# Perceiver block on one core: the last rows' normalisation ahead of the choice of experts, and clock-keeping products moved into two other waits

## What is computed

```python
x = x + xattn(layernorm(x), ctx_768)      # 16 heads, 257 context rows of 192 numbers a batch
x = x + local_attention(layernorm(x))     # each row attends to its neighbours at distance <= 2
x = x + experts(layernorm(x))             # 8 experts, each row goes to one
```

```python
router_logits = x @ Wr + br
expert_mask = one_hot(argmax(router_logits, axis=-1), 8)
for e in range(8):
    h = gelu(x @ W1[e] + b1[e])           # 256 to 1024
    h = gelu(h @ W2[e] + b2[e])           # 1024 to 512
    y = h @ W3[e] + b3[e]                 # 512 to 256
    out = out + expert_mask[:, e:e + 1] * y
```

## Time and profile before

| | |
|---|---|
| median of 3 runs | 704.46 us (704.05 to 704.51) |
| the profiled execution | 707.72 us |
| its span, first to last instruction | 706.0 us |
| TensorE busy | 686.0 us (97%) |
| VectorE busy | 473.8 us (67%) |
| ScalarE busy | 450.7 us (64%) |
| GpSimd busy | 437.7 us (62%) |
| mean granted TensorE clock | 0.992 |
| slices of 17.65 us in which TensorE is busy less than 90% | the first, the 24th and 25th (406 to 441 us), the last |

### The profile page before, as it was taken

One profiled execution on the slowest core, in us unless ns is written; L12 is line 12 of the kernel. 1 busy time (PEld: TensorE's weight loads), 2 busy tenths in 40 slices (PEclk: granted clock), 3 DMA queues, 4 the chain that ended last, 5 costly groups with the idle time before them and its releaser, 6 DMA issues.

```text
span 706.0 us, 26647 instructions
## 1 busy us (share of the span) xinstructions
PE 686.0 (97%) x9297; PEld 582.1 (82%) x9298; DVE 473.8 (67%) x1456; ACT 450.7 (64%) x1071; POOL 437.7 (62%) x596
## 2 busy tenths in 40 slices
PE   7999999999999999999999968999999999999996
PEld 6888888888888888888888756888888888888885
DVE  4467677777777777777798878999961991259001
ACT  4656666666766766666666644575757576666663
POOL 6475665655656565656555663677766776767553
PEclk9999999999999999999999997999999999999999
DMA  7432233333323333343458334239033541272100
GB/s 214 118 89 78 75 76 96 91 88 82 97 67 80 102 90 78 81 97 80 94 136 268 99 109 169 90 100 330 25 106 112 176 147 45 82 229 69 40 7 1
DMA packets 56178, 74.35 MB, mean 105 GB/s; under 512 B 6589, under 2 KB 41950, under 8 KB 56128
## 3 DMA queue, kind: packets, MB, share of 16 engines
q1 hardware_dynamic: 49792, 60.63, 31.2%
q0 software_dynamic: 2992, 8.26, 3.8%
q10 hardware_dynamic: 3344, 4.80, 1.9%
HBM read 67.30 MB, written 7.27 MB: 106 GB/s over the span
## 4 chain that ended last, share of the span: by engine, by line
PE 93%; DVE 2%; DMA 1%; issue 1%; POOL 1%; ACT 1%; SPq 0%; POOLq 0%; ACTq 0%; DVEq 0%
PE ps_s L2046 18%; PE ps_kv L1623 12%; PE ps_kv L1631 11%; PE ps_p L1709 8%; PE ps_o L1695 6%; PE ps_s L1642 6%; PE ps_p L1994 5%; PE ps_kv L1994 4%; PE ps_o L2060 4%; PE ps_s L2025 3%; PE ps_m L1828 2%; PE ps_m L1774 2%; PE ps_m L1747 2%; PE ps_m L1832 2%; PE ps_s L2054 1%
## 5 line engine op out<-in xcount | busy, mean ns | idle before, releaser
L877 ACT ACTIVATE prob<-prob,neg_max 128x257 f32<-128x257 f32 x256 | 111.2, 501 | 42.2 <-DVE neg_max L1122 40.6
L1122 DVE CUSTOM_DVE_ANT_0 prob<-ps_s,mask_add 128x257 f32<-128x257 f32 x256 | 94.7, 421 | 64.3 <-PE ps_s L1642 64.2
L1582 DVE CAST w<-w_raw 128x512 fp32r<-128x512 f32 x94 | 68.1, 725 | 57.1 <-DMA w_raw<-in_L_ffn_W_dram 57.1
L1585 DVE TENSOR_TENSOR w<-w_raw,w 128x512 fp32r<-128x512 f32 x112 | 103.1, 923 | 3.6
L685 POOL TENSOR_TENSOR ctx_parts<-ctx_raw,ctx_parts 128x512 fp32r<-128x512 f32 x64 | 82.9, 1295 | 23.8 <-ACT ctx_parts L872 21.9
L2046 PE MATMUL ps_s<-w,h_hi 128*128 x368 | 90.5, 397 | 0.0
L1631 PE MATMUL ps_kv<-wkv_hi,ctx_parts 128*128 128x256 f32 x512 | 84.6, 293 | 0.2 <-ACT kT L881 0.2
L1623 PE MATMUL ps_kv<-ctx_parts,wkv_hi 128*128 128x256 f32 x512 | 84.2, 292 | 0.3 <-POOL ctx_parts L685 0.2
L885 ACT COPY v<-ps_kv 128x512 f32<-128x512 f32 x64 | 37.5, 586 | 70.3 <-PE ps_kv L1631 70.3
L698 POOL COPY last_prob<-prob 128x4 f32<-128x4 f32 x64 | 12.3, 192 | 112.1 <-ACT prob L877 108.4
L813 POOL TENSOR_TENSOR h_lo<-h,h_hi 128x512 fp32r<-128x512 f32 x46 | 64.2, 1397 | 27.6 <-ACT h_hi L1017 21.4
(11 more groups left out here) (307 smaller groups left out, 1513.6 us busy)
## 6 DMA issues: line engine op xcount, KB each, us to landing
w_raw<-in_L_ffn_W_dram SPq DMA_DIRECT2D x24, 1024.0 KB, 7.2
ctx_raw<-in_ctx_turned_dram SPq DMA_DIRECT2D x63, 256.0 KB, 3.5
mask_add<-mask_dram SPq DMA_DIRECT2D x64, 128.5 KB, 3.4
w_raw<-in_L_ffn_W_dram SPq DMA_DIRECT2D x8, 512.0 KB, 4.0
rows_dram<-x3n ACTq DMA_DIRECT2D x15, 256.0 KB, 4.3
xt<-in_x_dram SPq DMA_DIRECT2D x16, 128.0 KB, 2.1
xr<-in_x_dram SPq DMA_DIRECT2D x16, 128.0 KB, 2.3
slot_x<-rows_dram,slot_ids POOLq DMA_INDIRECT x23, 4.0
```

Source lines behind the costliest of these rows:

```text
L877: a.activation(prob[:, g, :], prob[:, g, :], ACT.Exp, bias=neg_max[:, g:g + 1], scale=-1.0).then_inc(exp_done, 1)
L1122: d.tensor_tensor_reduce(prob[:, r, :], ps_s[r][:, 0:J], mask_add[:, k, :], -(HD ** -0.5), 3.0e38, ALU.add, ALU.min, neg_max[:, r:r + 1]). ...
L1582: d.tensor_copy(w[:, b, HI, part], raw[:, b, part]).then_inc(rounded, 1)
L1585: last = d.tensor_tensor(w[:, b, LO, part], raw[:, b, part], f32(w[:, b, HI, part]), ALU.subtract)
```

## The change

VectorE issues the normalisation of the last tile's rows directly behind the scaled logits, ahead of the choice of the expert, where it stood behind the choice. On TensorE the clock-keeping transposes behind the bias transpose become 20 instead of 5, five new ones stand between the counts and the last chunk sum, and those behind the product that finds the slots' tokens become 16 instead of 24: 41 in these places where there were 29. Nothing that is computed changes.

```diff
--- before.py
+++ after.py
@@ -1517,13 +1517,13 @@
                 match_single(2)
                 dve.wait_ge(raw_logits_done, 2)
                 scale_logits(t).then_inc(tail_taken, 1)
+                normalise(2, t, x3n[:, 0:D], x3n[:, D:2 * D], xn3_done)
 
             last_tile()
 
 
             dve.wait_ge(tail_taken, taken("logits"))
             choose_single(3)
-            normalise(2, TILES - 1, x3n[:, 0:D], x3n[:, D:2 * D], xn3_done)
             rank_single(3, ps_m[:, E:2 * E])
             totals = ps_m[:, 2 * E:3 * E]
             d.tensor_scalar(padded[:, :], totals, 1.0, float(P - 1), ALU.max, ALU.add).then_inc(route, 1)
@@ -1961,14 +1961,15 @@
                 pe.wait_ge(bias_in, 32)
                 n_b = E * (F1 + F2) // P
                 t.transpose(ps_s[3][:, 0:n_b], bias_rows[:, :], ident[0:n_b, 0:n_b]).then_inc(bias_turned, 1)
-                keep_clock(5)
+                keep_clock(20)
                 fill_chunks(2, 3, 4, 14)
                 rank_single(3, ps_m[:, E:2 * E])
                 count_all(ps_m[:, 2 * E:3 * E]).then_inc(ranked, 1)
+                keep_clock(5)
                 fill_chunks(15).then_inc(chunks_filled, 1)
                 pe.wait_ge(route, 7)
                 t.matmul(ps_kv[:, 0:SLOTS], chunk_tokens[:, :], of_slot[:, :], start=True, stop=True).then_inc(tokens_found, 1)
-                keep_clock(24)
+                keep_clock(16)
 
             last_tile()
```

## The result

| | before | changed |
|---|---|---|
| median of 9 runs | 704.51 us (704.04 to 706.15) | 706.58 us (703.95 to 707.73) |
| ratio of the times, 95% interval | | 1.0023 [1.0013, 1.0033] |
| the profiled execution (its span) | 707.72 us (706.0) | 706.0 us (704.3) |

The changed kernel is 0.23% slower, about 1.6 us, and scatters more.

The account below looks back on a forecast made before the run. It took TensorE, 93% of the chain, as the bound, so a gather shift counts one for one. Gather −0.48 plus clock +0.12 gave −0.36 us on the median 704.46: 704.1 us, range 703.1 to 705.2.

Parts of the forecast that it names:

- The normalisation ahead of the choice: VectorE, last tile: normalising directly behind the logits lands the rows sooner, so the first gather starts 0.48 us earlier.
- The 0.13 us that the insertion was to cost the ids: VectorE, choice of expert: the inserted normalisation makes `top`, the ranking and the ids 0.13 us later.
- The first rival (the ids hold it): First gather: it waits for the slots' ids, not the rows, so it starts 0.13 us later; 704.6 us, chance 0.32.
- The transposes ahead: TensorE before the ids: 20 and five transposes fit in existing waits, cost nothing; clock 1.00 in 421 to 422.
- the 16 in place of 24 and the clock: TensorE behind the ids' product: 16 transposes end at 426.1 or 427.3, within the gather wait; no clock gain counted.
- No instruction waits for them: TensorE behind the ids' product: the clock-keeping transposes lie in the wait for the gather and hold up nothing.
- I expect the lower level for layer 1 again: Layer 1 of slot 0: the clock is low again, so work starting 0.48 us earlier gives back 0.12 us.
- if the next six take more than 2: Sign of being wrong: the six products of layer 1's second half take more than 2 us.
- TensorE idle for 3 to 4 us: Before layer 1: with 16 transposes TensorE idles 3 to 4 us instead of 1.6.
- The price of a transpose at the lower level: TensorE behind the ids' product: 24 transposes in 4.65 us, so 0.19 us each at the lower clock.
- the clock comes back later: Layer 1, second half: low clock costs +1.5 us, with the gather unimproved +0.13; 706.1 us, chance 0.08.
- Putting the difference on the median: Whole kernel: durations came from the 707.72 us profiled execution, but the −0.36 us was applied to the 704.46 us median.

Follow-up runs that it names:

- the late store: Kernel before with 20 transposes instead of 5 behind the bias transpose and five new ahead of the last chunk sum, normalisation unmoved, expert number bounded: 1.0031 of before, 707.26 us.
- control: Kernel before plus only an assertion bounding the expert number that TensorE loads, an edit all variants carry: 1.0002 of before, 704.73 us.
- the filled kernel: Changed kernel, expert number bounded, transposes filling every wait (32, 10, 3, 32 behind the ids' product, 4 before layer 1): 0.9991 and 0.9986 of before, 704.29 and 704.18 us.

## Why the prediction was wrong

It said 704.1 us, 703.1 to 705.2, and gave slower by over 0.2% a chance of 0.07. It came out 0.23% slower, with a median of 706.58 us.

**The normalisation ahead of the choice** was right and somewhat better than costed: the gather came 0.59 us earlier (forecast 0.48). The 0.13 us that the insertion was to cost the ids was 0.02: `top` came 0.21 us later relative to the logits (0.54 against 0.33), but `chosen_single` lasted 0.24 us in place of 0.40. That the rows, not the ids, held the gather is shown by seven profiles with the edit (issue at 4.61 to 4.63) against six without it (5.20 to 5.22), and by the one with the late store (6.73). Where the edit is absent the gather starts 0.83 to 0.86 us after the store has landed, whether that is at 424.38 (control) or at 426.3 (the late store). The first rival (the ids hold it) is out.

**The transposes ahead** cost nothing on TensorE, as I said, and kept the clock full in 421 to 422. That 20 more of them are 40 instructions on TensorE, which are fetched through the same DMA engines as the rows, I did not count. In the changed kernel it does no harm, because the store has landed by 422.75 and the packet comes at 424.4; with the transposes alone the gather starts 1.5 us later (6.73 against 5.20).

**The step that failed is the one on the 16 in place of 24 and the clock.** "No instruction waits for them" was wrong: in the control the 24 are in the chain, and slot 0's transposes wait 0.6 us behind them. And "I expect the lower level for layer 1 again", priced at 0.12 us, took the lower level in the first profile for the kernel's ordinary state. It was not: in the control layer 1 runs at full clock, so there was 2.4 us to lose, and with 16 the kernel loses part of it in most runs: 2.32 and 2.08 us for the two halves in the changed kernel's profile, where the control has 1.65 and 1.40. The recorded sign of being wrong, "if the next six take more than 2", is what came.

The wait itself was mis-sized too. The prediction had TensorE idle for 3 to 4 us (its own terms give 2.6 to 3.8), since it took over the 5.00 us of the first profile's gather. The gather took 3.5 us, the idle time was 0.97 and 1.22 us in the two profiles, and the lower level came all the same. The price of a transpose at the lower level, 0.19 us, was the mean of 24 of which the last ran at full clock; with all but the last few at the lower level they took 5.21 us in the control, 0.22 each.

The rival "the clock comes back later" had the direction and half of the mechanism: the second half of layer 1 does run partly at the lower level (2.08 us). Its sum, 706.1 us, is close to what was measured, but by luck. It counted 1.5 us in the second half alone and a gather that had not improved; measured were 0.7 us in each half and a gather 0.6 us earlier, from a starting point 2.6 us lower. I gave it 0.08 with the argument that "little is left to lose". That argument was read off one execution.

**Putting the difference on the median** was the same fault: the text noted that the profiled execution was 3.26 us above it and did not ask where. Of that, 2.6 us lay in the very passage that was to be changed. With layer 1 at full clock as the starting point, a lower level through both halves is +2.4, and slot 0's transposes, which no longer stand behind the 24, start 0.9 earlier (8.22 against 9.10): slower by 1.5 us, where 1.6 was measured. That sum was made after the fact, and that it fits so well is luck in part: the changed kernel's two profiles lose 0.6 and 1.7 us in the passage against the control.

## What to carry to other kernels

Before costing a change to a passage, hold the profiled execution against the median of the runs: if it is some microseconds off, find where, since the state it shows may be the exception and the terms read from it have the wrong sign. Products that only keep the clock should reach nearly to the end of the wait and not beyond it (here ending 0.5 us short was best, and running 0.6 us over cost that much in the passage), and how long they last depends on the clock they are to keep (24 of them: 5.21 us in the control, 4.34 us where they began at full clock); if the waits ahead of them are filled too, the clock is full and their length can be set to the wait. Adding instructions can move the fetch of instructions, and what a transfer on the critical path costs then changes without any dependency (2.8 against 4.3 us here).

## What the runs showed of the hardware that I had not expected

- **A packet of instructions holds up a transfer.** One packet of some 16 KB, 0.98 us of one DMA engine, made a 128 KB store land in 4.3 us in place of 2.8. In the first profile of before there is such a packet just before 427.0, in the middle of the first gather, which took 5.0 us; in the thirteen other profiles it took 3.3 to 3.6. In the control the packet (428.0 to 428.5) came as the first gather ended and lies in the middle of the second, which took 4.1 us, against 3.5 to 3.8 in the twelve profiles other than these two. With the normalisation alone it came right behind the first gather's issue (424.5 to 425.0), before any of its data moved, and that gather took 3.4 us. So that the packet caused the 5.0 is likely, but only the store's case was put to a test, by moving the packet ahead of it. The Trainium skill, Runtime: NRT & Kernel Launch, Instruction fetch mechanics, says that instructions are fetched in blocks of 16 KiB, 256 instructions each, over a DMA queue; the size of the packet agrees (the page of the first profile has 30 of them, 0.49 MB in all), and that such a block delays other transfers is what these runs add.
- **The same store takes 1.7 or 2.8 us by its place.** The 128 KB took 2.8 us issued 1.57 us after the logits (4.3 us with the packet of instructions in it), and 1.7 to 2.0 us issued 0.65 us after them. GpSimd issues a gather of rows of x (line 787) 0.1 us after the logits in both cases; in the control its packets move among those of the store. That this is what slows the store was not tested.
- **Transposes alone raise and hold the clock.** In the control the clock rose from 0.50 (428 to 429) to 0.89 (429 to 430) and 1.00, with nothing but transposes of the unit matrix on TensorE from 424.11 to 429.32, and the filled kernel, with nothing else in the waits of the passage, has 1.00 there throughout and 0.996 to 1.000 over the run. The Trainium skill, TensorE: Matmul & The Clock Gate, Part 4, says that they do not count as busy; these runs do not agree. The same page says in its section HAM oscillation that a wait for DMA between bursts of products makes the next burst start cold. The kernels with none behind the ids agree: 4.04 and 4.53 us of waiting, and 2.92 us for the first half of layer 1.
- **The same kernel meets the clock's fall at different points.** With 16 behind the ids layer 2 started 16.65 us after the logits in one look and 18.27 in the other, with the same instructions. Over all profiles the idle time just before slot 0's transposes orders the outcomes but does not decide them. Where it was 0 to 0.52 us (five profiles), layer 1 ran at full clock throughout. Where it was 0.97 to 1.08 us, it did in three profiles and not in the fourth. Where it was 1.22 us or more (five profiles), it did in none. What decides it within an execution was not settled, and neither was the cause of the scatter of 1 us among runs of equal clock.
